# A 1x1 convolution computed from half-precision high and low parts, in a four-image attention block

## The reference

```python
out = bilinear_resize(x, 64, 64)
out = relu(bn1(conv1x1(out, conv1_w)))
q, k, v = three 1x1 convolutions of out, with bias (32, 32 and 256 channels)
attn = softmax(q^T k over all 4096 places)
out = gamma * (v attn^T) + out
out = relu(bn2(out))
out = bn3(conv1x1(out, conv2_w))
return relu(bilinear_resize(out, 128, 128) + x)
```

## Time and profile before

| | |
|---|---|
| median of three runs | 2378.29 us |
| profiled execution | 2376.7 us |
| its span in the trace | 2374.9 us |
| mean granted TensorE clock | 0.991 |
| HBM traffic | 135.24 MB read, 67.11 MB written |

### The profile page before, as it was taken

One profiled execution on the slowest core, in us unless ns is written; L12 is line 12 of the kernel. 1 busy time (PEld: TensorE's weight loads), 2 busy tenths in 40 slices (PEclk: granted clock), 3 DMA queues, 4 the chain that ended last, 5 costly groups with the idle time before them and its releaser, 6 DMA issues.

```text
span 2374.9 us, 48165 instructions
## 1 busy us (share of the span) xinstructions
PE 2298.0 (97%) x15970; PEld 1652.3 (70%) x15970; DVE 1813.8 (76%) x3326; ACT 1703.9 (72%) x3241; POOL 1681.2 (71%) x1610
## 2 busy tenths in 40 slices
PE   4799999999999999999999999999999999999998
PEld 2377777777667777777747777777765777777774
DVE  7766578887678888888677888888767777777778
ACT  5467777777647777777755777777764777777773
POOL 7992458888469988888727988889845454444465
PEclk8899999999999999999999999999999999999999
DMA  6321112223103322232301333233310122222322
GB/s 212 107 68 50 36 53 106 100 96 107 54 18 107 107 106 97 98 106 98 107 10 54 108 106 104 100 107 106 107 54 1 55 71 71 71 71 71 142 93 103
DMA packets 59273, 204.11 MB, mean 86 GB/s; under 512 B 8752, under 2 KB 9840, under 8 KB 59120
## 3 DMA queue, kind: packets, MB, share of 16 engines
q1 hardware_dynamic: 41696, 138.93, 18.2%
q10 hardware_dynamic: 17424, 63.45, 6.5%
...
HBM read 135.24 MB, written 67.11 MB: 85 GB/s over the span
## 4 chain that ended last, share of the span: by engine, by line
PE 88%; DVE 5%; POOL 3%; ACT 2%; issue 1%; SPq 1%; DMA 0%; DVEq 0%; ACTq 0%; POOLq 0%
PE acc L1145 19%; PE acc L1147 18%; PE acc L1146 18%; PE et L1021 10%; PE emx L1009 6%; PE wrk L1043 5%; PE acc L1071 4%; PE wrk L1009 3%; PE acc L1063 2%; PE wrk L1034 1%; DVE am L775 1%; DVE qs L767 1%; DVE ks L767 1%; PE acc L1055 1%; DVE mx L698 1%
## 5 line engine op out<-in xcount | busy, mean ns | idle before, releaser
L1145 PE MATMUL acc<-vh,ph 128*128 128x257 f16 x4096 | 1120.1, 273 | 1.7 <-DVE vl L781 1.4
L1147 PE MATMUL acc<-vh,pl 128*128 128x257 f16 x4096 | 1116.2, 273 | 0.0
L1146 PE MATMUL acc<-vl,ph 128*128 128x256 f16 x4096 | 1110.9, 271 | 0.0
L463 ACT ACTIVATE ph<-et 128x512 f16<-128x512 f32 x1024 | 611.7, 597 | 296.9 <-PE et L1021 287.9
L726 DVE TENSOR_TENSOR pl<-et,ph 128x512 f16<-128x512 f32 x1024 | 702.3, 686 | 146.4 <-ACT et L464 143.6
L464 ACT ACTIVATE et<-et 128x512 f32<-128x512 f32 x1024 | 607.9, 594 | 0.0
L1146 PEld LDWEIGHTS acc<-vl,ph 128*128 128x128 f16 x4096 | 400.9, 98 | 277.5 <-issue 20.5
L1145 PEld LDWEIGHTS acc<-vh,ph 128*128 128x128 f16 x4096 | 400.3, 98 | 70.7 <-issue 11.0
L1147 PEld LDWEIGHTS acc<-vh,pl 128*128 128x128 f16 x4096 | 395.5, 97 | 56.2
L377 POOL TENSOR_TENSOR ct<-cd,uw 128x512 f32<-128x512 f32 x246 | 325.3, 1344 | 124.9 <-DVE xres L757 119.3
L1021 PE MATMUL et<-qs,ks 98*128 (+1 forms) x1024 | 390.1, 381 | 1.5 <-DVE pl L726 0.9
...
## 6 DMA issues: line engine op xcount, KB each, us to landing
...
```

Of the source, the lines that this page charges most:

```text
L463: ops.activation(ph[:, t % 4, :], et[t % 2][:, :], ACT.Exp)
L1145: mm(acc[it][:, 0:C + 1], ph[:, tt % 4, pt], vh[:, tt, 0:C + 1], start=tt == 0, stop=False)
L1146: mm(acc[it][:, 0:C], ph[:, tt % 4, pt], vl[:, tt, :], start=False, stop=False)
L1147: last = mm(acc[it][:, 0:C + 1], pl[:, tt % 4, pt], vh[:, tt, 0:C + 1], start=False, stop=tt == JT - 1)
```

## The change

The second convolution is computed as the attention product is. Its input gets a half-precision high part `hh` and a low part `hl`, its weights `w2h` and `w2l`, and each of the two input halves takes three half-precision matmuls (high by high, high by low, low by high) in place of one in float32. To keep the parts in range, each input channel is scaled by a bound on its size, which is worked out once a batch from the bound on the values (`sizes_of_h`, `sum_of_h`); the weights are scaled to match once a batch (`scaled_convolution`), and bn3 undoes it.

- `relu_h`, on ScalarE, now makes two passes over each half: one writes `hh`, one overwrites `hbuf`.
- `low_h`, new on VectorE, subtracts them into `hl`: in steps 12 and 18 (5 and 8 in the last block), in a batch's entry after the first units of queries and keys for its predecessor's last chunk, and after the last block.
- `sizes_of_h` and `sum_of_h`, new on VectorE, and the unit `h_sum` on TensorE stand in the entry.
- `scaled_convolution` stands in steps 28 and 30 of a batch's first block.
- In the last block conv2 follows steps 10 and 12 instead of 9 and 11.

```diff
@@ -66,6 +67,15 @@
         pl = sb("pl", [P, 4, IB], F16)
         osb = sb("osb", [P, IT, C])
         hbuf = sb("hbuf", [P, CH, IB])
+        hh = sb("hh", [P, CH, IB], F16)
+        hl = sb("hl", [P, CH, IB], F16)
+        w2h = sb("w2h", [P, CH, C], F16)
+        w2l = sb("w2l", [P, CH, C], F16)
+        hs = sb("hs", [P, 16])
+        h_bound, h_inv, h_row, s2_abs, b2_abs, w2_max = (hs[:, 2 * i:2 * i + 2] for i in range(6))
+        h_all, h_all_inv, gam_abs, h_att = (hs[:, i:i + 1] for i in range(12, 16))
+        h_size = sb("h_size", [P, CH])
+        h_par = sb("h_par", [P, 3, CH])
...
@@ -473,8 +485,11 @@
 
             def relu_h(chunk, half):
                 act.wait_ge(ot_done, chunk * 2 + (half + 1))
-                ops.activation(hbuf[:, half, :], hbuf[:, half, :], ACT.Relu, bias=par[:, B2, half:half + 1],
-                               scale=par[:, S2, half:half + 1]).then_inc(h_rdy, 1)
+                act.wait_ge(h_scaled, chunk // NB + 1)
+                at_least(act, cv_rdy, chunk * 2)
+                scale, bias = h_par[:, 0, half:half + 1], h_par[:, 1, half:half + 1]
+                ops.activation(hh[:, half, :], hbuf[:, half, :], ACT.Relu, bias=bias, scale=scale)
+                ops.activation(hbuf[:, half, :], hbuf[:, half, :], ACT.Relu, bias=bias, scale=scale).then_inc(h_rdy, 1)
 
...
                 for dst, src in jobs + [(new[:, 1:BR + 1, :], cv)]:
-                    done = ops.activation(dst, src, ACT.Identity, bias=par[:, B3, half:half + 1], scale=par[:, S3, half:half + 1])
+                    done = ops.activation(dst, src, ACT.Identity, bias=par[:, B3, half:half + 1], scale=h_par[:, 2, half:half + 1])
                 done.then_inc(y_rdy, 1)
...
+            def low_h(chunk, half):
+
+                dve.wait_ge(h_rdy, chunk * 2 + (half + 1))
+                ops.tensor_tensor(hl[:, half, :], hbuf[:, half, :], hh[:, half, :], ALU.subtract).then_inc(hl_rdy, 1)
+
+            def sizes_of_h(b):
+
+                if b == 0:
+                    dve.wait_ge(par_ok, PAR_OPS)
+                    dve.wait_ge(wt_ok, 3)
+                    ops.scalar_tensor_tensor(s2_abs, par[:, S2, :], -1.0, par[:, S2, :], ALU.mult, ALU.max).then_inc(h_fixed, 1)
+                    ops.scalar_tensor_tensor(b2_abs, par[:, B2, :], -1.0, par[:, B2, :], ALU.mult, ALU.max).then_inc(h_fixed, 1)
+                    ops.scalar_tensor_tensor(gam_abs, gam[:], -1.0, gam[:], ALU.mult, ALU.max).then_inc(h_fixed, 1)
+                    ops.tensor_reduce(w2_max, w2t[:], AX.X, ALU.max, apply_absolute_value=True).then_inc(h_fixed, 1)
+                    dve.wait_ge(h_fixed, 4)
+                ops.tensor_scalar(h_att, vg[:, 0:1], gam_abs, None, ALU.mult).then_inc(h_step, 1)
+                dve.wait_ge(h_step, b * 10 + 1)
+                ops.tensor_scalar(h_bound, am1[:], h_att, None, ALU.add).then_inc(h_step, 1)
...
+                ops.tensor_tensor(h_size[:], h_bound, w2_max, ALU.mult).then_inc(h_size_rdy, 1)
+                ops.reciprocal(h_inv, h_bound).then_inc(h_step, 1)
+                dve.wait_ge(h_step, b * 10 + 6)
+                ops.tensor_scalar(h_inv, h_inv, H_TOP, None, ALU.mult).then_inc(h_step, 1)
+
+            def sum_of_h(b):
+
+                dve.wait_ge(h_sum, b + 1)
+                ops.tensor_scalar(h_all, wrk[:, C + 1:C + 2], 1e-30, None, ALU.max).then_inc(h_step, 1)
+                dve.wait_ge(h_step, b * 10 + 8)
+                ops.reciprocal(h_all_inv, h_all).then_inc(h_step, 1)
+                dve.wait_ge(h_step, b * 10 + 9)
+                ops.tensor_scalar(h_row, h_bound, h_all_inv, H_TOP, ALU.mult, ALU.mult).then_inc(h_step, 1)
+
+            def scaled_convolution(b, part):
+
+                if part == 0:
+                    dve.wait_ge(h_step, b * 10 + 10)
+                    at_least(dve, y_rdy, b * NB * 2)
+                    ops.tensor_scalar(h_par[:, 2, :], par[:, S3, :], h_all, 1.0 / (H_TOP * H_TOP), ALU.mult, ALU.mult)
+                    ops.tensor_tensor(h_par[:, 0, :], h_inv, par[:, S2, :], ALU.mult)
+                    ops.tensor_tensor(h_par[:, 1, :], h_inv, par[:, B2, :], ALU.mult).then_inc(h_scaled, 1)
+                    for h in range(CH):
+                        last = ops.tensor_scalar(w2h[:, h, :], w2t[:, h, :], h_row[:, h:h + 1], None, ALU.mult)
+                    last.then_inc(w2_hi, 1)
+                else:
+                    dve.wait_ge(w2_hi, b + 1)
+                    for h in range(CH):
+                        last = ops.scalar_tensor_tensor(w2l[:, h, :], w2t[:, h, :], h_row[:, h:h + 1], w2h[:, h, :], ALU.mult,
+                                                        ALU.subtract)
+                    last.then_inc(w2_rdy, 1)
+
...
                             first_down(i // 2 + 2)
+                        if i == 4 and not is_first(b):
+                            low_h(b * NB - 1, 0)
+                            low_h(b * NB - 1, 1)
                     elif kind == "qk":
                         if i < NB - 1:
                             largest_a(b, i)
...
@@ -857,6 +936,11 @@
                         pair_max(b, n + 1, units[0])
                     if c > 0 and t in (T_OT[0] + 1, T_OT[1] + 1):
                         residual(g - 1, n - 1, T_OT.index(t - 1))
+                    t_low = T_LOW_LAST if is_last(b, c) else T_LOW
+                    if c > 0 and t in t_low:
+                        low_h(g - 1, t_low.index(t))
+                    if c == 0 and t in T_SCALE:
+                        scaled_convolution(b, T_SCALE.index(t))
                     t_add = add_steps(g)
...
+            low_h(NB * B - 1, 0)
+            low_h(NB * B - 1, 1)
             add_piece(0, LATE - 1, 2)
             add_piece(0, LATE - 1, 3)
...
@@ -1035,12 +1121,15 @@
                 last.then_inc(ot_rdy, 1)
 
             def conv2(chunk, half):
-                pe.wait_ge(h_rdy, chunk * 2 + 2)
+                pe.wait_ge(hl_rdy, chunk * 2 + 2)
                 bank = wrk if not (isinstance(chunk, int) and chunk == NB * B - 1) else last_bank(half)
                 if half and bank is wrk:
                     pe.wait_ge(y_rdy, chunk * 2 + 1)
+                cs = slice(half * P, (half + 1) * P)
                 for h in range(CH):
-                    last = mm(bank[:, :], w2t[:, h, half * P:(half + 1) * P], hbuf[:, h, :], start=h == 0, stop=h == CH - 1)
+                    mm(bank[:, :], w2h[:, h, cs], hh[:, h, :], start=h == 0, stop=False)
+                    mm(bank[:, :], w2h[:, h, cs], hl[:, h, :], start=False, stop=False)
+                    last = mm(bank[:, :], w2l[:, h, cs], hh[:, h, :], start=False, stop=h == CH - 1)
                 last.then_inc(cv_rdy, 1)
 
...
+                        pe.wait_ge(h_size_rdy, b + 1)
+                        for h in range(CH):
+                            last = mm(wrk[:, C + 1:C + 2], ones_p[:, :], h_size[:, h:h + 1], start=h == 0, stop=h == CH - 1)
+                        last.then_inc(h_sum, 1)
...
+                        if c == 1 and t == t_cv[0]:
+                            pe.wait_ge(w2_rdy, b + 1)
                         conv2(g - 1, t_cv.index(t))
...
-        seq += [row, m[0], m[1], one, scale, m[2], qk, v[0], m[3], m[4], m[5], v[1], m[6], v[2], m[7], *v[3:6]]
+        seq += [row, m[0], m[1], one, scale, m[2], qk, v[0], m[3], sizes, m[4], m[5], v[1], m[6], v[2], norm, m[7], *v[3:6]]
     else:
-        seq += [v[0], m[0], m[1], row, qk, one, m[2], v[1], m[3], v[2], m[4], m[5], v[3], m[6], v[4], m[7], v[5]]
+        seq += [v[0], m[0], m[1], row, qk, one, m[2], v[1], m[3], v[2], m[4], m[5], v[3], m[6], v[4], total, m[7], v[5]]
     beside = {6: "shift", 8: "shift_rows", 10: "energies", 12: "energies", 14: "energies"}
     for i in range(6, VU):
         seq.append(v[i])
...
 FIRST_AFTER_CONV2 = min(_u for _u in _wrk_units if _u > EMAX_AT[T_CV[1]][0])
+T_LOW = (12, 18)
+T_LOW_LAST = (5, 8)
+T_SCALE = (28, 30)
...
@@ -1295,7 +1395,7 @@
 
 T_ADD_FIVE = ((1, 3, 4, 5), (7, 8, 10, 11), (13, 14, 16, 17), (20, 21, 22, 23), (27, 28, 29, 30))
 T_STORE_FIVE = (7, 13, 19, 26)
-T_CV_LAST = (9, 11)
+T_CV_LAST = (10, 12)
 T_ADD_LAST = ((1, 3, 4, 5), (7, 8, 9, 10), (11, 12, 13, 14), (19, 20, 21, 22), (23, 24, 25, 26), (27, 28, 29, 30))
 T_STORE_LAST = (7, 12, 16, 24, 28)
 

```

More of the change, by code:

```diff
@@ L35 @@
 V_TOP = 2.0 ** 14
+H_TOP = 2.0 ** 14
 BN = 1.0 / (1.0 + 1e-5) ** 0.5
@@ L94, in attention_block_kernel @@
         ws = sb("ws", [D, 2])
-        ones_d = sb("ones_d", [D, P])
+        ones_p = sb("ones_p", [P, P])
         even_f = sb("even_f", [P, 4])
@@ L133, in attention_block_kernel @@
         cv_rdy, y_rdy = sem("cv_rdy"), sem("y_rdy")
+        h_fixed, h_step, h_size_rdy, h_sum, h_scaled, w2_hi, w2_rdy, hl_rdy = (
+            sem(n) for n in ("h_fixed", "h_step", "h_size_rdy", "h_sum", "h_scaled", "w2_hi", "w2_rdy", "hl_rdy"))
         late_ld, late_zero, late_xy, late_stored = sem("late_ld"), sem("late_zero"), sem("late_xy"), sem("late_stored")
@@ L738, in residual @@
```

(29 more changed lines are left out.)

2 lines of the change are left out of this document (1 added, 1 removed).

## The result

The changed kernel takes 2428.01 us (median of 4 runs, 2424.65 to 2431.36), the kernel before 2379.43 beside it (4 runs, 2378.1 to 2382.97). The ratio is 1.0201, with an interval of 1.0188 to 1.0214: slower by 48.6 us, where I forecast +10. The direction was right. The size was off by a factor of five, and the time lies 30 us above my range.

The account below looks back on a forecast made before the run. It took TensorE, busy 97% of the span, as the bound. Terms: -26.7 + 17.3 + 5.4 + 2.7 + 1.4 + 0.5 + 1.6 + 5.7 + 2.2 = +10.1 us on 2376.7, giving 2386.8, or 2388 as median; range 2373 to 2398.

Parts of the forecast that it names:

- What conv2 gives back: conv2 on TensorE: six half-precision matmuls take 1.28 us instead of 1.71, saving 0.43 a call, 26.7 us over 62 calls.
- The second pass in steps 3 and 7: ScalarE's added `relu_h` pass, 0.72 us, delays TensorE: 17.3 us for step 3; 5.4, 2.7 and 1.4 for step 7.
- `low_h` in the blocks: VectorE in steps 12 and 18: idle time and lead cover it, 0 for all blocks; 0.5 us for the last block.
- Rival C: VectorE meets GpSimd more often through `low_h`, making `pl` late in steps 12 and 18: +14 us, 2402; chance 0.12.
- The entries: Batch starts: `sizes_of_h` on VectorE, `h_sum` on TensorE (3.2 us) and ScalarE's extra passes (1.4) cost 5.7 us together.
- Scaling the weights: End of a batch's first block: four VectorE instructions of 0.4 us each, 0.4 uncovered in 4 batches, 1.6 us.
- The last blocks of the batches: Each batch's last block: conv2's saving against ScalarE stalls of 0.18 us, twice in 4 blocks, 1.4 us; -1.5 in all.
- After the last block: Past block 31: two added passes and one `low_h` cost 2.1 us, conv2 gives back 0.7; taken as +2.2, ends 0.7 and 3.5.

Follow-up runs that it names:

- gain-alone kernel: The changed kernel with one pass of `relu_h`, no `low_h` (`hh` in its place), bounds in PSUM and weights scaled in the first batch only: 2356.82 us.
- the repaired one: The changed kernel with passes spread over steps 6, 11, 14, 17, a batch's last chunk out of the entry, bounds in PSUM, weight scaling moved: 2373.47 us.
- the bounds unheld: Two runs of the changed kernel: `sizes_of_h` with its bounds in PSUM, 2410.29 us; or split into one-wide instructions in SBUF, 2411.43 us.

## Why the prediction was wrong, by its steps

- **What conv2 gives back**: right. 1.29 us a call against 1.28. In the gain-alone kernel, which keeps `h_sum` (3.2 in the forecast), 22.8 of the 26.7 us reach the end.
- **The second pass in steps 3 and 7**: right in step 3, too high in step 7. In step 4 TensorE's unit starts 0.95 us later than the matmul before it needs (forecast 0.98), in 24 blocks; the group row above has 19.0 us of idle time for them. Around step 9 it stands 0.43 where it stood 0.32 (blocks 10, 12 and 20), so 0.11 where I had 0.30; in the last batch (block 28) 0.43 where it stood not at all, for my 0.45. If the other blocks are like these, that is 4.6 us for 8.1. Taking the pass away gives 26.5, and moving it 27.4.
- **`low_h` in the blocks**: this is the step that failed, "I take 0 for all blocks; the far end is 0.3 a step". The runs give 20.0 us in the changed kernel and 19.0 in the repaired one. It lasts 1.09 us on the mean, and 0.68 or 0.69 where no GpSimd instruction runs beside it; in blocks 1 and 2, where none does, 0 was right. The "good 1.3 us" of lead did not hold, because VectorE is late by more than one instruction: a sum close behind it takes 1.79 us (at 1011.43), and the delay is carried over two more steps. Rival C had this mechanism, at 14 us and a chance of 0.12, and even it stood for `low_h` alone; its condition, a `low_h` longer than the lead of 1.3, was too simple, since 1.67 cost less than 1.47 did.
- **The entries**: failed in "small dependent instructions of VectorE start 0.20 apart". That holds for the earlier trace rows, which are one element wide. The new ones are two wide; 4.9 us in the second entry, not 1.4. With the bounds unheld 16.6 to 17.7 us come back, where I had 5.7 for all of the entries.
- **Scaling the weights**: failed in "I estimate 0.4 each". Alone it is even less (0.61 for two). Beside GpSimd it is 2.73 for two, and 8.8 us in all instead of 1.6. I had taken the price of an instruction from its size, and the price of a meeting only for the long ones of the earlier trace rows.
- **The last blocks of the batches**: -0.71 in three, where the sum has -0.86 + 2 x 0.18 = -0.50, and +1.0 in block 31, where it has 0; together -1.1 for -1.5. **After the last block**: +3.1 for +2.2, inside its ends; the twelve matmuls ran at 0.43 each where I counted a gain of 0.7.

`low_h`, the entries and the scaling have one cause: a VectorE instruction of the held kind lasts longer by about what is left of GpSimd's instruction, and GpSimd is busy 55 of 61.6 us in a block. What that costs TensorE depends on what stands behind it.

The trace of the kernel before already showed it, in two small instructions near its start, which the prediction doesn't use.

```profile
26.90 1.26 POOL L344 TENSOR_TENSOR xin<-xin 128x512 f32<-128x512 f32 x1
27.00 1.17 DVE L691 TENSOR_TENSOR par<-par 128x2 f32<-128x2 f32 x1
...
28.21 0.16 DVE L693 TENSOR_TENSOR par<-par 128x2 f32<-128x2 f32 x1
```

Both are two wide with two tensors in SBUF. The first takes 1.17 us and ends where GpSimd's ends; the second starts with none running and takes 0.16.
